# First batch's query work of a two-stage attention kernel moved into the context stage, its products from fp32 to fp32r

## The chip, the cores and the metric

The kernel is one program on one core of a Trainium2 chip. Its engines run side by side: TensorE (PE, with its weight loads as PEld), VectorE (DVE), ScalarE (ACT), GpSimd (POOL) and the sync engine (SP), which issues nearly all DMAs. The metric is the device time of one execution in microseconds; lower is better. Three executions of the kernel before took 1945.25, 1947.76 and 1950.10 us, median 1947.76 us.

## The reference

Two layers over latents `x` (4 batches x 256 rows x 512) with a context of 1601 rows of 512 per batch. The change touches the first layer's attention alone:

```
C_q  = layernorm(x) @ Wq_d                  # 512 -> 64
C_kv = ctx @ Wkv_d                          # 512 -> 32
q    = (C_q @ W_qk)  as 16 heads of 32
attn = softmax(q . C_kv / sqrt(32)) over the 1601 context rows
x    = x + attn @ (C_kv @ Wv_u as 16 heads of 32)
```

Then follow a layer norm and a product with int4 weights, a grouped attention (16 heads, 4 groups, head size 96) over context and latents, and a mixture layer. The softmax subtracts a maximum for each row of scores, so the kernel computes scores twice: once as maxima, once as exponents.

## The kernel before

There are three functions, each a block that ends when all engines have reached its end, DMAs landed.

**First stage, `context_products`.** The context is cut in 16 pieces (4 per batch, 384 rows, the last of each batch 449). For each piece PE turns it (`turn`), ACT and DVE split it into a high and a low fp32r part, and PE makes three key groups (`keys_of`, 12 products each) and three or four value groups (`values_of`, 12 products each). Weights are turned between the value groups of pieces 1 to 12 (`("w", w)`). Groups take one of four PSUM banks in turn, and before PE opens a bank it waits until the group four places back has been read (`open_bank`). ACT reads a group first and DVE after it. `turn_c` turns 32 compressed columns, which are stored in `cst_scr` as the first layer's keys. The list `groups(n)` is the order of work for all engines. In its last pieces stand the turning of the first batch's normalised rows (`("x", 0)`, `("x", 1)`, in piece 13) and `C_q` (`("cq",)`, in piece 14). SP walks its own fixed order: at the head of iteration n the load of context piece n + 2 and `load_small(n)`, then the key stores of piece n, the compressed rows of n - 1, the weight loads for n + 1, the stores of turned output weights (`wo_out`, two buffers), the value store.

**Second stage, `latent_attention_and_ffn`.** Sixteen courses s = 0 to 15, four for each batch, each for one group of four heads. `before()` stands ahead of them: eight query products of batch 0 (`("a", 0, hp)`, two heads each, fp32, stationary `wqk` of 64 partitions), 32 maxima of course 0 (`("max", 0, i)`, one product of 400 columns and one DVE reduction each), the row of the maxima (`row`), and the first six maxima of course 1. A course interleaves 13 pairs of score products with 26 other items: the maxima of the course after it, and in some courses query products (`a`), `C_q` (`cq`), normalisation, products for the third stage. `course(s)` shares these out between the scores by a fixed count. These items use a ring of four banks as well. The score products use three banks that ACT empties by exponents; `values` follow two score pairs later. The stage starts with DMAs of batch 0's keys (`cst`, 600 KB) and values (`cv`).

**Third stage, `grouped_attention`**, uses `home[0]` and two more buffers for keys. The change only renames one of them.

"Piece" and "iteration" are counted from 0. A "v tile" is a value group; "read" means that ACT and DVE have both taken what they need.

Of the kernel before, what the change touches and what calls it, by code (L numbers as in the profile page):

```python
# [8 lines left out]
ALU = mybir.AluOpType  # L9
# [119 lines left out]
def build(nc, A, out):  # L129
# [10 lines left out]
    with ExitStack() as ctx:  # L140
# [9 lines left out]
        home = [sb(f"home{i}", [P, n], F32R) for i, n in enumerate((NK + 1, 2 * GC, NK + 1))]  # L150
        with ExitStack() as early:
            def weight(name, cols, dt=F32R):
# [6 lines left out]
                     (("bias0", [P, D]), ("wqd", [P, DC, LQ]), ("wqk", [LQ, H0, 3 * HD0]), ("wvu", [P, NG * 2, 2, HD0 + 1]),  # L159
                      ("cq", [LQ, T]))}  # L160
            context_products(nc, A, ident, negid, ps, ln, home, wkvh, wkvl, wqh, wql, w0T, w1T, *small.values(),
                             k_scr, v_scr, cst_scr, cv_scr, wo_scr)
            latent_attention_and_ffn(nc, A, ident, negid, ps, ln, home, wkvh, wkvl, wqh, wql, w0T, *small.values(),
                                     cst_scr, cv_scr, q_scr, k_scr, v_scr, x_scr)
        grouped_attention(nc, A, ident, negid, ps, ln, home, q_scr, k_scr, v_scr, x_scr, wo_scr, sum_scr, o_scr, w1T, out)

def context_products(nc, A, ident, negid, ps, ln, home, wkvh, wkvl, wqh, wql, w0T, w1T, bias0, wqd, wqk, wvu, cq,
# [15 lines left out]
    C0 = 3 * HD0  # L184

    with ExitStack() as ctx:  # L186
# [6 lines left out]
        cnat = sb("cnat", [P, 3, 3, D])  # L193
        ctail = sb("ctail", [P, D])
        xa = sb("xa", [P, TT, D])
# [7 lines left out]
        wd = sb("wd", [P, DC, HD0])  # L203
        w0i = sb("w0i", [P, DC, D], I32)
        w0s = sb("w0s", [P, DC, D // P])
        w0z = sb("w0z", [P, DC, D // P])
        w0n = w0i[:, :, :].bitcast(F32)
        xaT = w0n[:, 0:2, :].rearrange("p a (c m) -> p (a c) m", c=2)
        wo_out = sb("wo_out", [HD1, 2, 2, D], F32R)

        const = sem("const0")
        ctx_in = [sem(f"ctx_in{i}") for i in range(3)]
# [4 lines left out]
        w_small, xa_in, xa_done, step_a = sem("w_small_loaded"), sem("xa0_in"), sem("xa0_ready"), sem("dve_step0")  # L217
        done = {"act": sem("group_read_by_act"), "dve": sem("group_read_by_dve")}
# [16 lines left out]
        def groups(n):  # L235
# [16 lines left out]
        def last_reader(g):  # L252
            kind = g[0]
            if kind in ("x", "cq") or kind == "w" and F_0 <= g[1] < F_1:
                return "act"
# [40 lines left out]
        def _(sp):  # L296
# [18 lines left out]
            def load(n):  # L315
                b, p = divmod(n, NP)
                if n >= 3:
# [1581 lines left out]
```

## Time and profile before

| | us |
|---|---|
| median of three executions | 1947.76 |
| profiled execution, its own time | 1948.22 |
| its span, first to last instruction | 1946.4 |
| PE busy in the span | 1872.9 |
| DVE / ACT / POOL busy | 1019.9 / 904.3 / 655.7 |
| mean granted TensorE clock, share of full speed | 0.967 |

PE is busy 96% of the span, no other engine over 52%. A busy PE is not yet a PE at its peak: the second part of the page shows the granted clock in 40 slices, and two of them (the seventh and the eighth, 292 to 389 us) are at 0.6 and 0.8. In the timeline, each row has the start, the busy time, the engine and line, and in brackets how long the engine had been idle and what released it.

### The profile page before, as it was taken

Reading aid. Unit: us, or ns where it says so; the run is one execution under the profiler, and the core shown is the slowest. Engines: PE = TensorE matmul, PEld = TensorE weight load, DVE = VectorE, ACT = ScalarE, POOL = GpSimd, SP = SyncE. Lnnn points to the kernel's source line nnn. Section 1 sums busy time; section 2 is a strip of 40 time slices with the busy share of each in tenths; the row PEclk is TensorE's granted clock in tenths of the full one; section 3 lists DMA queues with packets and bytes.
Section 4 is the critical chain, followed back from the end, with each engine's and each line's share of the span. In section 5 each row is a group of like instructions: output and inputs, shape, how many; then the busy total and the mean of one; then the engine's idle time right before and its main releaser. Section 6 shows DMA issues by size and latency. Waiting matters only on the chain. (4 is left out here: it accounts for less than half of the span.)

```text
span 1946.4 us, 23155 instructions
## 1 busy us (share of the span) xinstructions
PE 1872.9 (96%) x8570; PEld 1337.1 (69%) x8570; DVE 1019.9 (52%) x1852; ACT 904.3 (46%) x1726; POOL 655.7 (34%) x630
## 2 busy tenths in 40 slices
PE   7999997999999999999979999999999999999998
PEld 6999894444465555555577777767777677777764
DVE  3464434667655565665635555554444645554415
ACT  2333331445334344444326666645666456655660
POOL 0000000000000000000017777755777577766770
PEclk9999996899999999999989999999999999999998
DMA  5978863000010111021058444544444355443201
GB/s 182 286 243 268 280 209 113 1 1 18 29 59 27 34 66 33 33 67 44 22 177 197 111 108 118 133 124 116 126 113 112 81 132 135 124 124 98 69 25 44
DMA packets 192950, 208.42 MB, mean 107 GB/s; under 512 B 87425, under 2 KB 157569, under 8 KB 192838
## 3 DMA queue, kind: packets, MB, share of 16 engines
q1 hardware_dynamic: 177124, 188.92, 34.1%
q10 hardware_dynamic: 15714, 18.03, 3.1%
q8 instruction: 68, 1.11, 0.2%
q14 instruction: 44, 0.36, 0.1%
HBM read 128.90 MB, written 77.94 MB: 106 GB/s over the span
## 5 line engine op out<-in xcount | busy, mean ns | idle before, releaser
L1475 POOL TENSOR_TENSOR pl<-pf,ph 128x512 fp32r<-128x512 f32 (+1 forms) x480 | 623.4, 1320 | 258.6 <-ACT pf L1669 258.6
L1666 ACT ACTIVATE ph<-ps 128x512 fp32r<-128x512 f32 (+1 forms) x480 | 288.4, 601 | 361.9 <-PE ps L1562 361.9
L1749 DVE TENSOR_REDUCE pm<-ps 128x1 f32<-128x464 f32 x480 | 307.7, 642 | 249.5 <-PE ps L1493 245.9
L1187 DVE TENSOR_REDUCE pm<-ps 128x1 f32<-128x400 f32 (+3 forms) x544 | 283.1, 572 | 96.9 <-PE ps L1020 84.0
L1080 ACT ACTIVATE pr<-ps 128x512 f32<-128x512 f32 (+1 forms) x416 | 219.1, 601 | 193.9 <-PE ps L952 192.9
L1669 ACT ACTIVATE pf<-ps 128x512 f32<-128x512 f32 (+1 forms) x480 | 289.7, 603 | 0.7 <-POOL pl L1475 0.7
L965 PE MATMUL ps<-pr,cv 128*64 128x512 f32 (+1 forms) x832 | 209.0, 618 | 0.0
L1580 PE MATMUL ps<-ph,vh 128*97 128x512 f32 (+1 forms) x480 | 193.0, 402 | 0.0
L1583 PE MATMUL ps<-pl,vh 128*97 128x512 f32 (+1 forms) x480 | 190.1, 396 | 0.8 <-POOL pl L1475 0.7
L1581 PE MATMUL ps<-ph,vl 128*97 128x512 f32 (+1 forms) x480 | 189.9, 396 | 0.0
L89 POOL TENSOR_SCALAR ln_v<-ln_mv 128x2 f32<-128x2 f32 x9 | 1.9, 214 | 507.1 <-DVE ln_mv L70 507.1
L1493 PE MATMUL ps<-kh,qh 96*128 96x464 f32 x320 | 121.3, 379 | 5.6 <-DVE pm L1749 5.6
L1560 PE MATMUL ps<-qh,kh 104*128 104x512 f32 x300 | 121.7, 406 | 0.0
L965 PEld LDWEIGHTS ps<-pr,cv 128*64 128x64 f32 (+1 forms) x832 | 51.9, 139 | 88.1 <-issue 59.9
L1583 PEld LDWEIGHTS ps<-pl,vh 128*97 128x97 f32 (+1 forms) x480 | 78.3, 163 | 36.0 <-POOL pl L1475 2.8
L930 POOL MEMSET home<- 96x1 f32 x1 | 0.1, 95 | 305.1 <-POOLq L186 305.1
L1581 PEld LDWEIGHTS ps<-ph,vl 128*97 128x97 f32 (+1 forms) x480 | 79.3, 165 | 27.1 <-issue 0.5
L1020 PE MATMUL ps<-home,ast 96*128 96x400 f32 (+1 forms) x256 | 91.1, 419 | 6.4 <-DVE pm L1187 3.2
L1580 PEld LDWEIGHTS ps<-ph,vh 128*97 128x97 f32 (+1 forms) x480 | 78.9, 164 | 25.1 <-issue 0.7
L1020 PEld LDWEIGHTS ps<-home,ast 96*128 96x128 f32 x256 | 50.3, 210 | 56.0 <-DVE pm L1187 25.8
L1020 PE MATMUL ps<-cst,ast 96*128 96x400 f32 (+1 forms) x256 | 83.1, 384 | 4.9 <-DVE pm L1187 3.5
L1020 PEld LDWEIGHTS ps<-cst,ast 96*128 96x128 f32 x256 | 46.0, 192 | 50.2 <-DVE pm L1187 28.2
(273 smaller groups left out, 3098.2 us busy)
## 6 DMA issues: line engine op xcount, KB each, us to landing
woT<-wo_turned SPq DMA_DIRECT2D x30, 768.0 KB, 6.1
v_scr<-vst SPq DMA_DIRECT2D x16, 1152.0 KB
cnat<-in_ctx_dram SPq DMA_DIRECT2D x16, 768.0 KB
q_scr<-qst SPq DMA_DIRECT2D x48, 256.0 KB, 2.5
vh<-v_scr SPq DMA_DIRECT2D x15, 672.0 KB
vl<-v_scr SPq DMA_DIRECT2D x15, 672.0 KB
home<-k_scr SPq DMA_DIRECT2D x14, 696.4 KB, 8.9
k_scr<-home SPq DMA_DIRECT2D x24, 384.0 KB, 7.8
```

The source lines that it names most:

```text
L965: mm = pe.matmul(bank(OB)[64 * half:64 * half + 64, :], cv[0:keys[kt], b % 2, kt, :], pr[0:keys[kt], n % NPR, half * BANK:(half + 1) * BAN ...
L1020: mm = pe.matmul(out[:, 0:k], queries, keys_t, start=True, stop=True)
L1080: act.activation(pr[0:keys[kt], n % NPR, half * BANK:(half + 1) * BANK], bank((2 * n + half) % SB)[0:keys[kt], :], ACT.Exp, scale=S0).then ...
L1187: dve.reduce_max(pm[:, j, ch:ch + 1], src[:, 0:(cuts if s < S else next_cuts)[ch][1]], AX)\
L1475: pool.tensor_tensor(pl[0:m, n % 2, cols], pf[0:m, half, :], ph[0:m, n % 2, cols].bitcast(F32), ALU.subtract).then_inc(plo, 1)
L1560: pe.matmul(out, kh[s % 3][:, k0:k0 + m], qh[s % 3][:, cols], start=True, stop=False)
L1580: pe.matmul(out, vh[0:m, s % 2, kt, :], ph[0:m, n % 2, cols], start=(kt == 0), stop=False)
L1581: pe.matmul(out, vl[0:m, s % 2, kt, :], ph[0:m, n % 2, cols], start=False, stop=False)
L1583: mm = pe.matmul(out, vh[0:m, s % 2, kt, :], pl[0:m, n % 2, cols], start=False, stop=(kt == KT - 1))
L1666: act.activation(ph[0:keys[kt], n % 2, cols], src, ACT.Exp, scale=S1).then_inc(phi, 1)
L1669: act.activation(pf[0:keys[kt], half, :], src, ACT.Exp, scale=S1).then_inc(exp_done, 1)
L1749: ins = dve.reduce_max(pm[:, j, ch:ch + 1], at[:, 0:cuts[ch][1]], AX)
```

## The change

- The first batch's first four query products (heads of groups 0 and 1), all 32 maxima of course 0 and their row go into the first stage: `a` into piece 13, maxima 8 to piece 13, 12 to piece 14, 12 to piece 15, the row after the last turning. `before()` is gone. The other four query products of batch 0 and the first maxima of course 1 are now items of course 0.
- The keys of batch 0 are loaded from `cst_scr` into a buffer of their own (`key0`) at iteration 6; queries have two tensors of two groups each (`ast0`, which also holds the turned output weights, and `ast1`).
- Query products are fp32r: `wqk` has 128 partitions, its upper half high parts and its lower half the low parts of the same weights, `cq` is written twice (partitions 0 to 63 and 64 to 127) and `cql` holds its low part. So each pair of fp32 products becomes four fp32r products, and `C_q` is computed twice, once for each half of the partitions.
- `wqk` is loaded at iteration 7 (six DMAs, where three stood at iteration 3), split by ACT and DVE after key group 2 of piece 8; the batch's rows are loaded at iteration 9 (was 2), turned in piece 11 (was 13), `C_q` comes in piece 12 (was 14). The context has two buffers of its own instead of three.

```diff
@@ context_products: groups(n)
             if n == N:
-                return [("c", N - 1)]
+                return [("c", N - 1), ("row",)]
             ws = list(weights_of(n))
-            order = [("k", n, 0), ("c", n - 1), ("k", n, 1), ("k", n, 2)]
+            first = {N - 3: [("a", hp) for hp in range(4)]}.get(n, [])
+            order = [("k", n, 0), ("c", n - 1)] + first[:1] + [("k", n, 1)] + first[1:2] + [("k", n, 2)] + first[2:3]
+            m0, m1 = {N - 3: (0, 8), N - 2: (8, 20), N - 1: (20, 32)}.get(n, (0, 0))
             for t, g in enumerate(tiles):
-                order += [g] + [("w", w) for w in ws[t:t + 1]]
-            if n == N - 3:
+                order += [g] + [("w", w) for w in ws[t:t + 1]] + (first[3:] if t == 0 else [])
+                lo, hi = [m0 + (m1 - m0) * u // len(tiles) for u in (t, t + 1)]
+                order += [("m", i) for i in range(lo, hi)]
+            if n == N - 5:
                 order += [("x", 0), ("x", 1)]
-            if n == N - 2:
+            if n == N - 4:
                 order += [("cq",)]
@@ SP
-                if n >= 3:
-                    sp.wait_ge(tp, DC * (n - 2))
+                if n >= 2:
+                    sp.wait_ge(tp, DC * (n - 1))
...
+                elif n == 6:
+                    sp.wait_ge(cs_st, 16 * NP)
+                    sp.dma_start(key0[0:HD1, 0:NC].bitcast(F32), cst_scr[0]).then_inc(key_in, 16)
+                elif n == 9:
+                    sp.wait_ge(wqk_lo, 1)
                     sp.dma_start(xa[:, :, :], A["x"][0].rearrange("(t p) d -> p t d", p=P)).then_inc(xa_in, 16)
...
-                elif n == 3:
-                    for r in range(3):
-                        sp.dma_start(wqk[:, :, r * HD0:(r + 1) * HD0],
-                                     A["L0_xattn_W_qk"].rearrange("l (h e) -> l h e", e=HD0)).then_inc(w_small, 16)
+                    sp.wait_ge(*turned(("w", F_1 - 1)))
+                    for half in range(2):
+                        for r in range(3):
+                            sp.dma_start(wqk_in[half * LQ:(half + 1) * LQ, :, r * HD0:(r + 1) * HD0],
+                                         A["L0_xattn_W_qk"].rearrange("l (h e) -> l h e", e=HD0)).then_inc(w_qk, 16)
@@ PE, first stage
+            def latent_keys(hp):
+                out = open_bank(("a", hp))
+                if hp == 0:
+                    pe.wait_ge(*read(("cq",)))
+                for j in range(2):
+                    pe.matmul(out[0:HD1, j * T:(j + 1) * T], wqk[:, 2 * hp + j, :], cq[:, :], start=True, stop=False)
+                    mm = pe.matmul(out[0:HD1, j * T:(j + 1) * T], wqk[0:LQ, 2 * hp + j, :], cql[:, :], start=False, stop=True)
+                mm.then_inc(product, 1)
+
+            def first_max(i):
+                out = open_bank(("m", i))
...
+                pe.matmul(out[:, 0:k], ast0[0:HD1, j * P:(j + 1) * P], key0[0:HD1, k0:k0 + k], start=True, stop=True)\
+                    .then_inc(product, 1)
@@ ACT, first stage
+                    elif g[0] == "a":
+                        act.wait_ge(*turned(g))
+                        if g[1] == 0:
+                            for i in range(2):
+                                act.wait_ge(o_st[i], 32 * (F_END - F_O) // 2)
+                        act.copy(ast0[0:HD1, g[1] * BANK:(g[1] + 1) * BANK], bank_of(g)[0:HD1, :]).then_inc(a_hi, 1)
...
+                    if g == ("k", 8, 2):
+                        act.wait_ge(w_qk, 16 * 6)
+                        act.copy(wqk[:, :, :], wqk_in).then_inc(wqk_hi, 1)
@@ second stage
-            extra, tail = {LEAD + 2: [("raise", s - 1)]} if s else {}, []
+            extra, tail = {LEAD + 2: [("raise", s - 1)]} if s else {5 * i + 4: [("a", 0, 4 + i)] for i in range(4)}, []
...
-            for i in range(LEAD, NI):
+            for i in range(LEAD if s else 0, NI):
                 main += extra.get(i, []) + maxima(s + 1, i, i + 1)
...
-        def before():
-            out = [("a", 0, 0), ("a", 0, 1)] + maxima(0, 0, 2)
-            for hp in range(2, 8):
-                out += [("a", 0, hp)] + maxima(0, 5 * hp - 8, 5 * hp - 3)
-            return out + [("row", 0)] + maxima(1, 0, LEAD)
...
                     for c in range(DC):
-                        mm = pe.matmul(out[0:LQ, 0:T], wqd[:, c, :], xaT[:, c, :], start=(c == 0), stop=(c == DC - 1))
+                        for half in range(2):
+                            mm = pe.matmul(out[half * LQ:(half + 1) * LQ, 0:T], wqd[:, c, :], xaT[:, c, :],
+                                           start=(c == 0), stop=(c == DC - 1))
                 elif g[0] == "a":
                     if g[1] and g[2] == 0:
                         pe.wait_ge(*read(("cq", g[1])))
                     for j in range(2):
-                        mm = pe.matmul(out[0:HD1, j * T:(j + 1) * T], wqk[:, 2 * g[2] + j, :], cq[:, :],
-                                       start=True, stop=True)
+                        pe.matmul(out[0:HD1, j * T:(j + 1) * T], wqk[:, 2 * g[2] + j, :], cq[:, :], start=True, stop=False)
+                        mm = pe.matmul(out[0:HD1, j * T:(j + 1) * T], wqk[0:LQ, 2 * g[2] + j, :], cql[:, :],
+                                       start=False, stop=True)
```

How the order moves on PE, at the border of the first two stages. Before: L490 is the last turning of the compressed rows (`turn_c`), the branches are the border, L1043 the query products, L1020 the maxima.

```order
L479 MATMUL ps<-wkvh,xl 65x416 x4
L490 MATMUL ps<-ident,cn 96x128 x3
L490 MATMUL ps<-ident,cn 96x65
L186 UNCONDITIONAL_BRANCH
L941 UNCONDITIONAL_BRANCH
L1043 MATMUL ps<-cq,wqk 96x256 x4
L1020 MATMUL ps<-home,ast 128x400 x2
L1043 MATMUL ps<-cq,wqk 96x256 x2
L1020 MATMUL ps<-home,ast 128x400
L1020 MATMUL ps<-home,ast 128x402
L1020 MATMUL ps<-home,ast 128x400 x3
```

After: L551 is a maximum of course 0 in the first stage, L557 the row, L1030 the first scores, L1099 the maxima of course 1, L1124 and L1125 the two parts of a query product.

```order
L502 MATMUL ps<-wkvh,xl 65x416 x4
L551 MATMUL ps<-key,ast 128x400 x2
L551 MATMUL ps<-key,ast 128x402
L513 MATMUL ps<-ident,cn 96x128 x3
L513 MATMUL ps<-ident,cn 96x65
L557 MATMUL ps<-ident,mx 8x128
L190 UNCONDITIONAL_BRANCH
L1019 UNCONDITIONAL_BRANCH
L1030 MATMUL ps<-ast,key 128x512 x2
L1099 MATMUL ps<-key,ast 128x400
L1030 MATMUL ps<-ast,key 128x512 x2
L1099 MATMUL ps<-key,ast 128x400 x2
```

The query products and the maxima between the border and the first scores are gone, and three of the maxima stand behind the last v tile.

On PE in piece 14 after the change: L502 are the 12 products of a v tile, L551 the four maxima that follow each tile.

```order
L502 MATMUL ps<-wkvh,home 128x416 x4
L551 MATMUL ps<-key,ast 128x400 x3
L551 MATMUL ps<-key,ast 128x402
L502 MATMUL ps<-wkvh,home 128x416 x4
L502 MATMUL ps<-wkvl,home 128x416 x4
```

Before, v tiles stood there without anything between them.

On SP, at the head of iteration 7, first before the change, then after it: L320 and L332 are the load of context piece 9, L374 and L394 the key stores of piece 7.

```order
L391 DMA v_scr<-vst 128x2x1152
L320 DMA cnat<-in_ctx_dram 128x3x512
L374 DMA k_scr<-home 128x2x449 x2
L374 DMA k_scr<-kst 128x2x449
L331 DMA cst_scr<-cs 96x384
```

```order
L411 DMA v_scr<-vst 128x2x1152
L332 DMA cnat<-in_ctx_dram 128x3x512
L367 DMA bias<-in_L_ffn_bias_dram 128x512
L372 DMA w0i<-in_L_xattn_W_qk_dram 64x16x32 x6
L394 DMA k_scr<-home 128x2x449 x2
L394 DMA k_scr<-kst 128x2x449
```

Seven DMAs have come between the load of the context and the key stores.

## Rows read from the trace of the kernel before

**Rows 1.** The page: busy time of PE, and the granted clock in 40 slices.

```profile
PE 1872.9 (96%) x8570; PEld 1337.1 (69%) x8570; DVE 1019.9 (52%) x1852; ACT 904.3 (46%) x1726; POOL 655.7 (34%) x630
...
PEclk9999996899999999999989999999999999999998
```

**Rows 2.** Timeline, border of the stages: start, busy us, engine, line, idle before.

```profile
298.94 0.91 PE L479 MATMUL ps<-wkvh,xl 128*65 128x416 f32 x4
...
308.40 3.70 PE L1043 MATMUL ps<-cq,wqk 64*96 64x256 f32 x8 [6.57 <-PEq L186]
...
312.00 0.80 POOL L934 MEMSET cv<- 128x832 f32 x1
...
346.89 0.67 PEld L952 LDWEIGHTS ps<-ast,home 104*128 104x128 f32 x2
```

**Rows 3.** Timeline, one turn of `before()`: query product, five maxima, the next.

```profile
319.10 2.02 PE L1043 MATMUL ps<-cq,wqk 64*96 64x256 f32 x4
...
322.49 2.50 DVE L1187 TENSOR_REDUCE pm<-ps 128x1 f32<-128x401 f32 x5
...
323.75 2.02 PE L1043 MATMUL ps<-cq,wqk 64*96 64x256 f32 x4
```

**Rows 4.** Windows: length, busy of PE, PEld, DVE, ACT, POOL, PEclk, DMA share, GB/s.

```profile
18.00:20.00 2.00, 0.64 (x6) 0.40 (x5) 0.56 (x1) 0.48 (x1) 0.00 (x0) 1.00 0.99 323
...
22.00:24.00 2.00, 0.09 (x1) 0.12 (x1) 1.76 (x3) 0.50 (x2) 0.00 (x0) 0.97 0.90 334
...
352.00:353.00 1.00, 1.00 (x7) 0.35 (x8) 1.00 (x2) 0.54 (x2) 0.00 (x0) 1.00 0.00 0
...
314.00:342.00 28.00, 27.43 (x56) 14.14 (x54) 18.60 (x35) 3.49 (x6) 0.00 (x0) 0.50 0.24 71
```

**Rows 5.** Timeline, piece 13: end of one v tile, its reads, end of the next.

```profile
259.50 0.91 PE L479 MATMUL ps<-wkvh,xl 128*128 128x416 f32 x4
...
260.45 0.48 ACT L570 CAST vst<-ps 128x384 fp32r<-128x384 f32 x1 [1.80 <-PE ps L479]
...
261.43 0.25 DVE L650 COPY cn<-ps 128x96 f32<-128x96 f32 x1
...
261.78 0.91 PE L479 MATMUL ps<-wkvh,xl 128*128 128x416 f32 x4
```

**Rows 6.** Timeline of PE in courses 0 and 2: `values` (L965), a query product, a maximum.

```profile
360.08 1.94 PE L965 MATMUL ps<-pr,cv 128*64 128x512 f32 x8
...
364.17 1.94 PE L965 MATMUL ps<-pr,cv 128*64 128x512 f32 x8
...
449.43 1.94 PE L965 MATMUL ps<-pr,cv 128*64 128x512 f32 x8
...
452.33 1.10 PE L1043 MATMUL ps<-cq,wqk 64*96 64x256 f32 x4
453.36 0.45 PE L1020 MATMUL ps<-cst,ast 96*128 96x400 f32 x1
...
454.39 1.94 PE L965 MATMUL ps<-pr,cv 128*64 128x512 f32 x8
```

**Rows 7.** Timeline of PE: fp32r products of 256 columns, for the third stage.

```profile
543.71 0.63 PE L974 MATMUL ps<-xth,wqh 128*128 128x256 f32 x4
544.18 0.63 PE L974 MATMUL ps<-xth,wql 128*128 128x256 f32 x4
```

**Rows 8.** Timeline of SP's queue: loads of `wqk`, and output weights in iteration 8.

```profile
72.25 7.75 SPq L352 DMA_DIRECT2D wqk<-in_L_xattn_W_qk_dram  x3
...
171.94 6.32 SPq L387 DMA_DIRECT2D wo_turned<-wo_out  x6
```

**Rows 9.** Waits of ACT, 0 to 310 us: us in total, times, longest us.

```profile
ACT wo_out L557 <- DMA wo_turned<-wo_out: 16.7, 4, 6.5
```

**Rows 10.** Windows, iteration 7: columns as in rows 4.

```profile
140.00:158.00 18.00, 18.00 (x105) 16.56 (x105) 8.21 (x15) 5.46 (x10) 0.00 (x0) 1.00 0.72 230
```

**Rows 11.** Timeline of PE: `C_q` of batch 0, fp32.

```profile
280.87 1.94 PE L507 MATMUL ps<-w0i,wqd 128*64 128x256 f32 x8
```

More of the change, by code:

```diff
@@ L253, in last_reader @@
             kind = g[0]
-            if kind in ("x", "cq") or kind == "w" and F_0 <= g[1] < F_1:
+            if kind == "x" or kind == "w" and F_0 <= g[1] < F_1:
                 return "act"
@@ L526, in _ @@
                         latent_queries()
+                    elif g[0] == "a":
+                        latent_keys(g[1])
+                    elif g[0] == "m":
+                        first_max(g[1])
+                    elif g[0] == "row":
+                        first_row()
                     else:
@@ L675, in group @@
                     c_lo(g[1])
+                elif g[0] == "cq":
+                    dve.wait_ge(cq_hi, 1)
+                    dve.tensor_tensor(cql[:, :], bank_of(g)[0:LQ, 0:T], cq[0:LQ, :], ALU.subtract).then_inc(done["dve"], 1)
+                elif g[0] == "a":
+                    lo = ast0[2 * HD0:3 * HD0, g[1] * BANK:(g[1] + 1) * BANK]
+                    dve.wait_ge(a_hi, g[1] + 1)
+                    dve.tensor_tensor(lo, bank_of(g)[2 * HD0:3 * HD0, :], lo, ALU.subtract).then_inc(done["dve"], 1)
+                elif g[0] == "m":
+                    i = g[1]
+                    dve.wait_ge(*turned(g))
+                    dve.reduce_max(pm[:, i // KC, i % KC:i % KC + 1], bank_of(g)[:, 0:cuts[i % KC][1]], AX)\
+                        .then_inc(done["dve"], 1)
+                    if i == QT * KC - 1:
+                        dve.wait_ge(*read(g))
+                        dve.reduce_max(mx[:, :], pm[:, :, :], AX).then_inc(mx_done, 1)
+                elif g[0] == "row":
+                    dve.wait_ge(*turned(g))
+                    shift_rows(dve, ast0[HD1:HD1 + QT, 0:GC], bank_of(g)[0:QT, 0:P], negid).then_inc(done["dve"], 1)
+                if g == ("k", 8, 2):
+                    dve.wait_ge(wqk_hi, 1)
+                    dve.tensor_tensor(wqk[LQ:2 * LQ, :, :], wqk_in[LQ:2 * LQ, :, :], wqk[LQ:2 * LQ, :, :], ALU.subtract)\
+                        .then_inc(wqk_lo, 1)
             line = iter([(n, g) for n in range(N + 1) for g in groups(n)])
@@ L827, in items @@
         def items():
-            yield from before()
             for s in range(S):
@@ L1037, in ring_item @@
                     for c in range(DC):
-                        mm = pe.matmul(out[0:LQ, 0:T], wqd[:, c, :], xaT[:, c, :], start=(c == 0), stop=(c == DC - 1))
+                        for half in range(2):
+                            mm = pe.matmul(out[half * LQ:(half + 1) * LQ, 0:T], wqd[:, c, :], xaT[:, c, :],
+                                           start=(c == 0), stop=(c == DC - 1))
                 elif g[0] == "a":
@@ L1057, in ring_item @@
                 mm.then_inc(product, 1)
-            for g in before():
-                ring_item(g)
             for s in range(S):
@@ L1107, in ring_item @@
                     act.copy(qst[:, u % 2, 0, 0:width(u)].bitcast(F32R), src[:, 0:width(u)]).then_inc(qhi, 1)
-            for g in before():
-                ring_item(g)
             for s in range(S):
```

140 lines of the change are left out of this document (83 added, 57 removed).

## The prediction

> **What bounds the kernel now.** I read the page first: PE is busy 96% of the span, and the granted clock has two low slices [rows 1]. Then the windows around those slices, the timeline of the border between the first two stages, and the timelines of the places that the change touches. From 308.40 us, where the second stage begins, to 346.89, where the weights of the first score are loaded, lies `before()`: 38.5 us without one score [rows 2]. It runs in turns of 4.65 us (319.10 to 323.75), a query product and five maxima, and the clock is at 0.50, the 1.2 GHz level, although PE shows 27.4 us busy of 28 [rows 3, 4]. In each turn PE has 3.4 us of columns (4 instructions of 512 column passes, 5 of 400, at 1.2 GHz); the rest is the ring, where DVE's 2.50 us for five maxima and the ACT and DVE reads of the product follow each other. At 352 us, in the first scores, the clock is back at 2.4 GHz. So the same work costs twice there what it would cost elsewhere, and this is what the change aims at. In the first stage PE is the bound: 18.0 of 18 us in iteration 7, DVE 8.2 [rows 10]. The v tiles of piece 13 follow each other without a gap [rows 5].
>
> **The change part by part.**
>
> *The stretch that goes.* After the border the first score waits only for POOL, whose memset of `cv` takes 0.80 us [rows 2]; in the new order it comes first on POOL, then a small one. I put the first score 1.1 us behind the border: 38.5 - 1.1 = 37.4 us gone. The keys are there already; `cv` is needed four score pairs later, some 5 us, for 192 KB issued first.
>
> *What comes into pieces 13 to 15.* A v tile takes 2.28 us (259.50 to 261.78); its products end at 260.41, its reads at 261.68, so 1.27 us later [rows 5]. Behind the tile PE now opens banks for maxima, and the bank four places back decides. With three items between two tiles, the next tile waits until this one is read: 1.3 us, of which the maxima use about 0.6. With four items (piece 14), it waits for the first maximum too, one DVE reduction of 0.50 us (2.50 for five [rows 3]): 1.27 + 0.5 + 0.1 = 1.87. Piece 13: three query products between key groups, about 0.5 each, and three tiles at 1.3: 5.4. Piece 14: 3 x 1.87 = 5.6. Piece 15: three tiles at 1.3; behind the last tile only its turning and the store count, delayed by DVE's three reductions, 0.6: 4.5. Sum 15.5 us. The cheapest it can be is the columns alone, 32 x 400 and 16 x 256 at 2.4 GHz, 7 us; the dearest is that nothing overlaps, 32 reductions of 0.5 and 4 products read in turn, 22. The row (one DVE operation) lies beside the stores and the border and costs nothing; without that cover it would cost its PE, DVE and waiting time, 1.5. ACT's copy of the first query product must wait until the last turned weights are stored; I count nothing, since PE can go on for three groups, and 3 us if it can't.
>
> *Query products in fp32r.* One in fp32 takes PE 1.03 us (452.33 to 453.36) and is not hidden: two score pairs with `values` take 4.96 us with it (449.43 to 454.39) and 4.09 with maxima alone (360.08 to 364.17) [rows 6]. Four fp32r products of 256 columns take 0.47 (543.71 to 544.18) [rows 7], so each of the 24 of batches 1 to 3 gives 0.56; I take 13 us in all. Least: a unit cannot go under 4.09, and if the other stationary shape or the switch costs 0.2 more, 24 x 0.3 = 7. Most: 0.7 each with the neighbours' transitions, 17.
>
> *`C_q` twice.* Eight fp32 instructions take 1.87 us of 1.94 [rows 11], sixteen would take 3.74. But the two halves use different 64-column halves of the array, as the halves of `values` do: those are eight instructions of 512 columns in 1.94 us [rows 6], while a single one of 256 takes 0.23, so they run in pairs. Between 0 and 1.9 for each of four; I take 0.3 each, near the row of `values`, 1.3 us in all.
> The Trainium skill (TensorE: Matmul & The Clock Gate, section Part 3: Packing small matmuls) says the same of small stationary operands, that matmuls on different column groups run concurrently, with 2.38 times for three groups; by its factor the two halves would cost 0.6 more each time, 2 us in all instead of 1.3. No row here shows the case with 256 columns.
>
> *Course 0.* It gets 36 items where it had 26: six more maxima and four query products at 0.5. A unit of 4.09 us has slack, since one with four maxima and one with five take the same, so half of the maxima are free: 4 x 0.5 + 3 x 0.25 = 2.8 us. From 1 to 5. It starts at 1.2 GHz as before; before, `before()` had run ahead of it, and the clock rose 5 us into the course. From a standing start I add 0.5 us, up to 2.
>
> *DMAs.* Six loads of `wqk` come into iteration 7, ahead of the key stores. Three took SP 7.75 us [rows 8], so six about 15.5. Iteration 7 has slack: the DMA share is 0.72 of 18 us [rows 10], 5 us of transfer. Six loads need some 8 us of transfer, the bias and the rows 2.5. From iteration 8 on there is hardly any: six stores of turned weights hold SP 6.3 us [rows 8], and ACT waits 16.7 us for them in four waits, the longest 6.5 [rows 9]. What iteration 7 does not absorb arrives there, about 5 us, part of it under work in ACT's wait. I take 3 us; from 0 to 12. The split of `wqk` (1536 columns, three times the 0.5 us that ACT takes for 384 to 512, as an estimate 1.5 to 2 us on ACT and DVE each) lies under the v tiles of piece 8. Two context buffers cost nothing: SP reaches iteration n after the tiles of n - 1, when piece n has long been turned.
 The trace agrees as far as it goes, 7.75 us of issue for 384 KB.
>
> *Sum*, against the profiled execution of 1948.2 us: -37.4 - 13 + 15.5 + 2.8 + 0.5 + 1.3 + 3 = -27.3, so 1920.9. The median of the runs is 0.5 below the profiled one: 1920.5 us. Own range of this case, 1911 to 1929.
>
> **The rivals.**
>
> *The DMA queue becomes the bound of pieces 8 to 12.* The third of the `wqk` loads, not the first, sets the pace: with nearly 5 us each SP would lose 29 us, not 15.5, and the key and value stores of piece 7 would come 13 us late. PE can run about 8 us ahead on its four banks. For it: the waits of rows 9, which already reach 6.5 us, and each PE gap there also sends the clock down. Against it: the share of 0.72. It costs 10 us more and 2 for the clock: 1932.
>
> *The fp32r products give nothing in place.* If a unit is held by the exponents and not by PE, the 13 us go to 3: 1930. Against it: 4.96 against 4.09 us.
>
> *The ring overlaps better.* If DVE reads maxima ahead of the tile and the tiles wait less, pieces 13 to 15 cost 9 and not 15.5: 1914. Against it: DVE keeps the order of the list.
>
> *Slower: the clock falls in pieces 13 to 15.* PE's load there drops to about 70% of its columns, which is what `before()` had, and that stayed at 0.50 for all of its length [rows 4]. If the waits behind each v tile let it fall and it doesn't rise, ten tiles and nine key groups, 43 us of work, take twice that, less 8 us that the waits absorb: 35 us more, 1956. It decides as soon as a wait of 1.3 to 1.9 us is enough for a fall. Against it: at 18 to 20 us PE is busy 0.64 us of 2 and the clock stays at 1.00; only in 22 to 24, with 0.09 us busy of 2, does it begin to fall, to 0.97 [rows 4]. And key groups follow without gaps.
> [...]
>
> **How the numbers follow.** The forecast 0.66; the DMA queue 0.17; fp32r without effect 0.05; better overlap 0.06; slower 0.06, with the clock and mishaps of its kind. The predicted time is the forecast's, 1920.5. For the range I take the better overlap and its own uncertainty at the low end, 1909, and the DMA rival with most of its spread at the high one, 1935; outside remain the clock's case and the ends of the others. A measurement of this kernel can tell about 0.3%, 6 us, from no change: faster than that in all cases but the last and the worst end of the DMA case, 0.91; within it 0.03; slower 0.06.
>
> **What would show it.** Right: the first scores about 1 us after the border; the border 18 to 20 us later than at 308.4; v tiles in piece 14 at intervals of 4.1 to 4.2 us, in piece 15 at 3.6; query products at half a microsecond or less in courses 2 to 11; a clock at 1.00 in pieces 13 to 15. Wrong: ACT's wait on the turned weights well over 20 us, or a new ACT wait on key or value stores in piece 8 (DMA rival); units with a query product still at 4.9 us; PEclk at 0.5 ahead of the border; a border later than 335 us.

## The result and the profile after

Four executions of the changed kernel took 1929.73 to 1935.98 us, median 1931.70; four of the kernel before, in the same session, had a median of 1946.62. The ratio is 0.9923, with an interval of 0.9908 to 0.9937: 15 us faster, where 27 were forecast (1920.5), and inside the range of 1909 to 1935. In a later session six more executions of the same changed kernel had a median of 1938.61 (1928.18 to 1944.83), ratio 0.9952 [0.9931, 0.9972]; the experiment with the fp32 products looks at the difference. Over the ten runs the median is 1936.8, so that the second session and the whole lie just outside the range.

The page of the changed kernel, its span 1931.3 us, its own time 1933.15, mean granted clock 0.981:

```profile
PE 1851.9 (96%) x8602; PEld 1328.5 (69%) x8602; DVE 1021.2 (53%) x1857; ACT 905.1 (47%) x1727; POOL 656.0 (34%) x630
...
PEclk9999998999999999999989999999999999999999
```

The slices at 0.6 and 0.8 of [rows 1] are one at 0.8: the long slow stretch is gone. The timeline of PE at the border (L551 maxima, L513 the turning of the compressed rows, L557 the row, L1030 the first score), which answers to [rows 2], and of POOL, whose start marks the border:

```profile
321.33 0.72 PE L551 MATMUL ps<-key,ast 96*128 96x400 f32 x3
322.90 0.56 PE L513 MATMUL ps<-ident,cn 128*96 128x128 f32 x4 [0.85 <-DVE cn L715]
324.56 0.37 PE L557 MATMUL ps<-ident,mx 128*8 128x128 f32 x1 [1.10 <-DVE mx L755]
330.96 1.22 PE L1030 MATMUL ps<-ast,key 104*128 104x512 f32 x2 [6.03 <-POOL cv L1011]
```
```profile
329.91 0.80 POOL L1010 MEMSET cv<- 128x832 f32 x1 [324.69 <-POOLq L190]
```

The first score comes 1.05 us behind the border, and the border has gone from 308.40 to 329.91: 21.5 us, where the prediction had 18 to 20. A v tile of piece 14 with its maxima, then the next tile (L502), to be read against [rows 5]:

```profile
286.71 0.92 PE L502 MATMUL ps<-wkvh,home 128*128 128x416 f32 x4
...
288.97 0.71 PE L551 MATMUL ps<-key,ast 96*128 96x400 f32 x3
290.46 0.45 PE L551 MATMUL ps<-key,ast 96*128 96x402 f32 x1 [0.78 <-DVE cn L715]
290.94 1.03 PE L502 MATMUL ps<-wkvh,home 128*128 128x416 f32 x4
```

The fourth maximum waits until DVE has taken the tile's compressed columns (L715); from tile to tile it is 4.23 us (4.35 for the next two), where 2.28 stood. In piece 15, with three maxima, it is 3.78 to 3.87. A query product is now four fp32r instructions, two with 128 rows of weights and two with 64. In piece 13 the four of these products take 1.15, 1.14, 1.06 and 1.06 us each, and not 0.47. In the courses it is 1.07 (L1124 with 128 rows of weights, L1125 with 64), and this is a whole unit, from one `values` (L1043) to the next, to be read against [rows 6]:

```profile
437.91 1.94 PE L1043 MATMUL ps<-pr,cv 128*64 128x512 f32 x8
...
440.72 0.28 PE L1124 MATMUL ps<-cq,wqk 128*96 128x256 f32 x1
440.93 0.35 PE L1125 MATMUL ps<-cql,wqk 64*96 64x256 f32 x1
441.22 0.36 PE L1124 MATMUL ps<-cq,wqk 128*96 128x256 f32 x1
441.50 0.35 PE L1125 MATMUL ps<-cql,wqk 64*96 64x256 f32 x1
441.79 0.45 PE L1099 MATMUL ps<-home,ast 96*128 96x400 f32 x1
...
442.82 1.94 PE L1043 MATMUL ps<-pr,cv 128*64 128x512 f32 x8
```

The unit is 4.91 us where [rows 6] have 4.96. These units are unlike (4.2 to 5.9 us), so each has to be compared with its own counterpart: batches 1 to 3 have 18 of them with query products and no other item but maxima. With one product (15 units) a unit is 0.04 to 0.07 us shorter after the change, with two (3 units) 0.04 to 0.07 longer, together 0.7 us less for 21 products; the median is 4.96 before and 4.90 after. Units with maxima alone are at 4.09 in both.

Windows of the changed kernel in pieces 13, 14 and 15, then shortly after the first score (length, busy time of PE, PEld, DVE, ACT, POOL, the granted clock, DMA share, GB/s):

```profile
255.00:278.00 23.00, 21.76 (x115) 18.24 (x111) 11.63 (x21) 7.46 (x14) 0.00 (x0) 1.00 0.54 169
278.00:300.00 22.00, 19.28 (x105) 17.31 (x106) 12.93 (x28) 4.97 (x9) 0.00 (x0) 1.00 0.32 117
300.00:322.00 22.00, 19.66 (x99) 17.02 (x97) 9.96 (x22) 3.89 (x8) 0.00 (x0) 1.00 0.34 125
334.00:335.00 1.00, 1.00 (x5) 0.70 (x3) 0.80 (x2) 0.56 (x3) 0.00 (x0) 0.62 1.05 393
335.00:336.00 1.00, 1.00 (x6) 0.49 (x4) 0.58 (x1) 0.59 (x2) 0.00 (x0) 1.00 1.03 387
```

The clock stays at full speed through the waits behind the tiles, and is back 4 to 5 us after the first score. `C_q`, twice as many instructions as in [rows 11], and ACT's wait on turned weights, which answers to [rows 9]:

```profile
253.35 1.95 PE L531 MATMUL ps<-w0i,wqd 128*64 128x256 f32 x16
```
```profile
ACT ast L612 <- DMA wo_turned<-ast: 18.8, 4, 5.9
```

### The profile page after: what moved, and what is told of

It is laid out like the page before. It is cut to its first block and busy times, and to the rows that moved or that the text cites. A ratio compares the mean times of both kernels' runs of the same rounds, so it can differ in the third digit from the quotient of the medians.

```text
span 1931.3 us, 23231 instructions
## 1 busy us (share of the span) xinstructions
PE 1851.9 (96%) x8602; PEld 1328.5 (69%) x8602; DVE 1021.2 (53%) x1857; ACT 905.1 (47%) x1727; POOL 656.0 (34%) x630
## 5 line engine op out<-in xcount | busy, mean ns | idle before, releaser
L1265 DVE TENSOR_REDUCE pm<-ps 128x1 f32<-128x400 f32 (+3 forms) x512 | 267.0, 572 | 92.3 <-PE ps L1099 79.4
L1043 PE MATMUL ps<-pr,cv 128*64 128x512 f32 (+1 forms) x832 | 208.3, 619 | 0.0
L1043 PEld LDWEIGHTS ps<-pr,cv 128*64 128x64 f32 (+1 forms) x832 | 51.0, 139 | 87.1 <-issue 59.5
L1099 PE MATMUL ps<-home,ast 96*128 96x400 f32 (+1 forms) x256 | 83.1, 383 | 7.0 <-DVE pm L1265 4.9
L1030 PE MATMUL ps<-ast,key 104*128 104x512 f32 (+1 forms) x208 | 76.8, 432 | 7.8 <-POOL cv L1011 6.0
L1099 PEld LDWEIGHTS ps<-home,ast 96*128 96x128 f32 x256 | 45.8, 191 | 52.1 <-DVE pm L1265 27.9
L1641 PE MATMUL ps<-home,key 104*128 104x512 f32 x180 | 73.9, 411 | 5.0 <-PEq L799 4.9
L1030 PE MATMUL ps<-ast,home 104*128 104x512 f32 (+1 forms) x208 | 75.1, 423 | 1.7
L1099 PE MATMUL ps<-key,ast 96*128 96x400 f32 x224 | 71.5, 379 | 3.5 <-DVE pm L1265 2.5
```

The source lines that it names most:

```text
L1043: mm = pe.matmul(bank(OB)[64 * half:64 * half + 64, :], cv[0:keys[kt], b % 2, kt, :], pr[0:keys[kt], n % NPR, half * BANK:(half + 1) * BAN ...
L1099: mm = pe.matmul(out[:, 0:k], queries, keys_t, start=True, stop=True)
L1265: dve.reduce_max(pm[:, j, ch:ch + 1], src[:, 0:(cuts if s < S else next_cuts)[ch][1]], AX)\
L1641: pe.matmul(out, kh[s % 3][:, k0:k0 + m], qh[s % 3][:, cols], start=True, stop=False)
```

## The experiments

The forecast failed in the price of the query products, so the first experiments ask what makes four fp32r instructions of 256 columns take up to 0.29 us each where [rows 7] have 0.12.

**Both fp32r products on 128 rows.** Low part of `C_q` on all 128 partitions, so that no weight load has 64 rows. It adds one term (low part times low part) to the sum.

```diff
-                      (... ("cq", [2 * LQ, T]), ("cql", [LQ, T]), ...)}
+                      (... ("cq", [2 * LQ, T]), ("cql", [2 * LQ, T]), ...)}
-                    mm = pe.matmul(out[...], wqk[0:LQ, 2 * hp + j, :], cql[:, :], start=False, stop=True)
+                    mm = pe.matmul(out[...], wqk[:, 2 * hp + j, :], cql[:, :], start=False, stop=True)
-                    dve.tensor_tensor(cql[:, :], bank_of(g)[0:LQ, 0:T], cq[0:LQ, :], ALU.subtract)
+                    dve.tensor_tensor(cql[:, :], bank_of(g)[:, 0:T], cq[:, :], ALU.subtract)
```

> The changed kernel, with the low part of C_q kept on all 128 partitions, so that both fp32r products of a query product have a stationary of 128 rows (it adds the product of the two low parts, which is tiny). In the changed kernel a query product takes 1.15 us, 0.29 for each instruction, where I had forecast 0.47. Theory A, the alternation of 128 and 64 rows costs about 0.17 us at each switch: a query product takes 0.5 to 0.6 us, the 28 of courses 0 to 15 give 14 to 18 us, with the four of the first stage 2 more, some of it taken by the exponents' pace: median near 1916, 1912 to 1920. Theory B, the stationary of 96 columns or the moving of cq is slow by itself: 0.29 stays and the time stays at 1930 to 1933. Theory C, the query products are hidden behind the exponents: they become shorter, the time does not change.

Measured: 1917.97 us (1913.39 to 1918.76), ratio to the kernel before 0.9851 [0.983, 0.9871]. Timeline of PE in this kernel:

```profile
432.83 0.28 PE L1124 MATMUL ps<-cq,wqk 128*96 128x256 f32 x1
432.95 0.28 PE L1125 MATMUL ps<-cql,wqk 128*96 128x256 f32 x1
433.06 0.28 PE L1124 MATMUL ps<-cq,wqk 128*96 128x256 f32 x1
433.18 0.28 PE L1125 MATMUL ps<-cql,wqk 128*96 128x256 f32 x1
433.31 0.35 PE L1099 MATMUL ps<-home,ast 96*128 96x400 f32 x1
```

The same four instructions now take 0.48 us, the 0.47 of [rows 7], and a unit with them 4.28 us (median of the same 18); over the 21 products the units lose 13.5 us against the changed kernel. The columns and the order are the same; what has changed is the height of two of the four weight loads, and of `cql` with it. Theory B falls (0.12 apart, not 0.29), and so does Theory C (the units became shorter too). The weight loads (PEld) show where the time goes. First the load for a 64-row product and the product itself in the changed kernel, then the same for its 128-row counterpart here:

```profile
440.93 0.16 PEld L1125 LDWEIGHTS ps<-cql,wqk 64*96 64x96 f32 x1 [0.28 <-issue]
440.93 0.35 PE L1125 MATMUL ps<-cql,wqk 64*96 64x256 f32 x1
```
```profile
432.83 0.16 PEld L1125 LDWEIGHTS ps<-cql,wqk 128*96 128x96 f32 x1
432.95 0.28 PE L1125 MATMUL ps<-cql,wqk 128*96 128x256 f32 x1
```

With all heights at 128 the load starts with the product before, 0.12 us ahead of its own. At a change to or from 64 rows it isn't ahead (440.93 for both, and within 0.01 us the same at 441.21, 441.50 and 441.79), so the load is no longer hidden. Why it isn't made ahead there, no run shows. Theory A, the change of height, is what fits.

**Two changes of height instead of four.** The order is high, low, low, high.

```diff
-                for j in range(2):
-                    pe.matmul(out[...], wqk[:, 2 * hp + j, :], cq[:, :], start=True, stop=False)
-                    mm = pe.matmul(out[...], wqk[0:LQ, 2 * hp + j, :], cql[:, :], start=False, stop=True)
+                for j, low in ((0, 0), (0, 1), (1, 1), (1, 0)):
+                    w, q = (wqk[0:LQ, 2 * hp + j, :], cql[:, :]) if low else (wqk[:, 2 * hp + j, :], cq[:, :])
+                    mm = pe.matmul(out[...], w, q, start=(low == j), stop=(low != j))
```

> The changed kernel with the four products of a query product in the order high, low, low, high: two switches between 128 and 64 rows inside instead of three. Theory A (a switch costs 0.17 us): 0.98 instead of 1.15 us, the neighbouring low products 0.12 apart; 28 times 0.17 is up to 5 us: 1927 to 1931. Theory B2 (any stationary of 64 rows costs 0.29, switch or not): no change in pace or time.

Measured: 1927.68 us (1925.32 to 1928.66), ratio 0.9904 [0.9885, 0.9922]. Timeline of PE:

```profile
435.63 0.28 PE L1125 MATMUL ps<-cq,wqk 128*96 128x256 f32 x1
435.84 0.47 PE L1125 MATMUL ps<-cql,wqk 64*96 64x256 f32 x2
436.24 0.36 PE L1125 MATMUL ps<-cq,wqk 128*96 128x256 f32 x1
436.43 0.34 PE L1099 MATMUL ps<-home,ast 96*128 96x400 f32 x1
```

0.80 us, and the unit 4.53 (median of the 18). With no change to or from 64 rows the product takes 0.47, with two 0.80, with four 1.07: 0.17 us for each of the first two and 0.14 for each of the others. It fell by more than was expected. One expectation failed: the two low products are 0.20 us apart (435.84 and 436.03) and not 0.12, though the weights of the second were loaded ahead (435.92). So the price of a change is spread over the next two products. Theory B2, that 64 rows cost 0.29 with or without a change, falls all the same.

**The query products in fp32, all else moved.** This tells what the move alone is worth.

```diff
-                    pe.matmul(out[...], wqk[:, 2 * hp + j, :], cq[:, :], start=True, stop=False)
-                    mm = pe.matmul(out[...], wqk[0:LQ, 2 * hp + j, :], cql[:, :], start=False, stop=True)
+                    mm = pe.matmul(out[...], wqk[0:LQ, 2 * hp + j, :], cq[0:LQ, :], start=True, stop=True)
```

> The changed kernel with its query products in fp32 again (one product of 64 rows where two of fp32r were), all that was moved stays moved. If the fp32r form gives nothing, as 1.15 us against 1.03 says, the time stays within 3 us of the changed kernel's 1932 and the whole gain belongs to the move. The courses with four query products are 1.7 us shorter after the change, which speaks for 5 us: then 1935 to 1938. My forecast of 13 us for this part would give 1945.

Measured: 1941.07 us (1932.18 to 1942.92, ten runs), ratio 0.9966 [0.9951, 0.998]. The product is `435.75 1.10 PE L1124 ... x4`, ended by the next maximum at 436.78: 1.03 us, as before; the unit 4.95 (median of the 18), and each unit is within 0.01 us of the same unit of the kernel before. By the medians fp32r would be worth 9 us, by the paired units 0.7 for 21 products, 0.8 for 24. (The 2 us in the next expectation come from medians over unlike units.) The two kernels were run again, in one session:

> The changed kernel once more, unaltered, on one chip with the fp32 version below, to settle how much the fp32r products as the change has them are worth. In the traces a unit of a course with a query product takes 4.87 us in this kernel and 4.95 in the fp32 version; over 24 products that is 2 us in place, and four products in the first stage are 0.1 us dearer each. Theory F (only that is real, the 9 us between the two medians were chance between runs): this kernel 2 to 4 us below the fp32 version, both with the same mean clock. Theory G (the fp32 version also has the clock fall more often: 0.977 mean against 0.981 in the runs so far, and 0.004 of 1934 us is 7.5 us): 7 to 10 us below it, again with 0.003 to 0.004 more clock. I expect G, 1932 us here.

> The changed kernel with its query products in fp32, as in the experiment with the fp32 products before, once more beside the unaltered changed kernel. Theory F: 2 to 4 us above it at the same clock, about 1935. Theory G: 7 to 10 us above it at a mean clock lower by 0.003 to 0.004, about 1941.

Measured: the unaltered changed kernel 1938.61 us (1928.18 to 1944.83), ratio 0.9952 [0.9931, 0.9972]; the fp32 version 1936.46 (1931.04 to 1941.76), ratio 0.9951 [0.9934, 0.9968]. No difference can be seen, so Theory G falls; 1 or 2 us, as by Theory F, are below what was resolved. Over both sessions the medians are 1936.8 (10 runs) and 1940.3 (16 runs), with mean clocks of 0.9785 and 0.9778. The fp32r products, as the change has them, are worth about 1 us by the units, and the medians can't say more.

The repeat also shows what differs from execution to execution. These are windows of the changed kernel in its first profiled execution (span 1931.3), then in the second (span 1943.0):

```profile
324.00:335.00 11.00, 4.41 (x12) 3.38 (x12) 3.85 (x7) 2.70 (x7) 2.46 (x4) 0.53 0.68 207
...
503.00:504.00 1.00, 0.36 (x1) 0.10 (x1) 0.96 (x3) 0.66 (x2) 0.00 (x0) 1.00 0.03 8
505.00:509.00 4.00, 4.00 (x14) 2.29 (x14) 1.50 (x4) 2.17 (x4) 2.73 (x14) 0.57 0.00 0
```
```profile
199.00:207.00 8.00, 6.81 (x22) 6.71 (x23) 7.10 (x16) 3.65 (x7) 0.00 (x0) 0.57 0.75 224
...
329.00:347.00 18.00, 12.36 (x31) 7.07 (x32) 5.46 (x9) 4.92 (x10) 2.47 (x4) 0.53 0.71 199
...
512.00:513.00 1.00, 0.24 (x3) 0.20 (x2) 0.97 (x3) 0.34 (x1) 0.00 (x0) 1.00 0.03 8
513.00:521.00 8.00, 8.00 (x26) 4.27 (x26) 5.31 (x16) 2.17 (x4) 2.74 (x14) 0.57 0.00 0
```

Adding up (1 - granted clock) over all windows of 1 us in which it was under 0.97 gives 36.9 us in the first execution and 52.5 in the second, as the mean clocks of 0.981 and 0.973 also say. The difference is 15.6, that of the spans 11.7. The same kernel has more or fewer such stretches, and they are longer or shorter. They are large enough for the scatter; that they are all of it is not shown, since part of each stretch is time in which PE waits anyway.

**The maxima two by two.** In pieces 14 and 15 maxima also stand behind the key groups, and never more than two between tiles.

```diff
-            m0, m1 = {N - 3: (0, 8), N - 2: (8, 20), N - 1: (20, 32)}.get(n, (0, 0))
+            ms = iter([("m", i) for i in {N - 3: range(0, 6), N - 2: range(6, 18), N - 1: range(18, 32)}.get(n, ())])
...
+            order = [("k", n, 0), ("c", n - 1)] + first[:1] + ahead() + [("k", n, 1)] + first[1:2] + ahead() \
+                + [("k", n, 2)] + first[2:3] + ahead()
             for t, g in enumerate(tiles):
-                lo, hi = [m0 + (m1 - m0) * u // len(tiles) for u in (t, t + 1)]
-                order += [("m", i) for i in range(lo, hi)]
+                order += two()
```

> The changed kernel with the 32 maxima of the first stage spread two to each value and key group of pieces 13 to 15 (6, 12, 14) instead of three or four behind value groups alone. Same work. If the waits for the ring of four banks make these pieces long, as ten waits of about 0.77 us in the trace say, they go: 8 us less, in pieces 14 and 15 2 to 2.5 us between the end of one tile's products and the next tile's start become 0.5; median near 1924. If the maxima cost PE time itself (three in 0.71 us), the time stays within 2 us.

Measured: 1927.68 us (1924.66 to 1928.90), ratio 0.9903 [0.9884, 0.9922]. Timeline of PE in piece 14 and at the border (L509 v tiles, L558 maxima, L1037 the first score):

```profile
289.93 0.91 PE L509 MATMUL ps<-wkvh,home 128*128 128x416 f32 x4
...
292.19 0.53 PE L558 MATMUL ps<-key,ast 96*128 96x400 f32 x2
292.56 0.92 PE L509 MATMUL ps<-wkvh,home 128*128 128x416 f32 x4
...
324.82 1.22 PE L1037 MATMUL ps<-ast,key 104*128 104x512 f32 x2 [6.67 <-POOL cv L1018]
```

From tile to tile it is 2.63 us instead of 4.23, with no wait: two maxima cost their 0.37. The first score comes at 324.82 where it was at 330.96, 6.1 us earlier. From `C_q` to the first score it is 71.0 us instead of 77.6, so 6.6 us of what pieces 13 to 15 cost were waits on the ring and not work. The larger part was work: 32 maxima of 0.185 us (5.9) and the four query products (4.4).

**The weights in two loads of whole rows.** Pieces of 2 KB instead of six loads in pieces of 128 bytes; ACT's copy repeats each head three times.

```diff
-                        for r in range(3):
-                            sp.dma_start(wqk_in[half * LQ:(half + 1) * LQ, :, r * HD0:(r + 1) * HD0], ...)
+                        sp.dma_start(w0n[half * LQ:(half + 1) * LQ, 0, :], A["L0_xattn_W_qk"])
```

> The changed kernel with W_qk loaded in two DMAs of whole 2 KB rows instead of six with pieces of 128 bytes; ACT and DVE make the three copies when they split it. DMA theory: the 2.4 us by which piece 13 starts later than before, beyond the moved turning and C_q, come from these loads; ACT's waits on the turned weights and value stores (29.7 us in the changed kernel, 23.8 before) fall back and 2 to 3 us are gone: 1929. Rival: the lag comes from the clock or from the moved rows load; no change within 1 us.

Measured: 1934.80 us (1932.47 to 1936.16), ratio 0.9926 [0.9912, 0.9941]. `C_q` comes at 251.43 where it was at 253.35, and the first score at 329.01 where it was at 330.96. That looks like 1.9 us for the loads, but SP's queue shows otherwise, first in the changed kernel, then in this one (L332 is the load of a context piece, at iteration 3; L372 and L371 are the loads of `wqk`, at iteration 7):

```profile
71.98 0.47 SPq L332 DMA_DIRECT2D cnat<-in_ctx_dram  x1
...
141.79 9.20 SPq L372 DMA_DIRECT2D w0i<-in_L_xattn_W_qk_dram  x6
```
```profile
70.08 0.47 SPq L332 DMA_DIRECT2D cnat<-in_ctx_dram  x1
...
139.88 2.04 SPq L371 DMA_DIRECT2D w0i<-in_L_xattn_W_qk_dram  x2
```

This execution was 1.9 us ahead at 70 us, 70 us before the edit does anything, and was 1.9 us ahead at `C_q` still. In the nine profiles of kernels with six loads `C_q` starts at 252.3 to 257.1, so 1.9 us is within what one execution differs from the next; PE's waits between 130 and 250 us add up to 6.9 us with six loads and 6.8 with two. ACT's wait on turned weights is listed as 16.4 us and not 18.8, but a fourth wait at the same line, of 2.4 us, is only put down to another releaser. So the DMA theory falls: the six loads hold SP for 9.2 us instead of 2.0, and cost nothing that can be seen. The rival in the expectation, no change, holds; whether the moved load of the rows or something else makes the lag was not separated.

**The wait on POOL moved to the first values.** The scores of course 0 don't need the memset of `cv`.

```diff
@@ scores
-                if kt == 0 and s == 0:
-                    pe.wait_ge(const, 2)
@@ values
+                if kt == 0 and s == 0:
+                    pe.wait_ge(const, 2)
```

> The changed kernel with PE's wait for POOL's memsets of cv moved from the first scores to the first values. The first scores start 1.0 us earlier after the border and the stage ends 1 us earlier: 1931. If what comes after (values waiting for cv, exponents) is late anyway, nothing.

Measured: 1932.22 us (1928.42 to 1938.04), ratio 0.9919 [0.9893, 0.9944]. From the row to the first score it is 5.36 us (323.50 to 328.86) instead of 6.40, so the first score comes 1.0 us earlier, as expected; the time shows nothing.

**All four together.** Its edit is those of the tall products, the spread maxima, the two loads and the late wait.

> The changed kernel with four edits together: both fp32r products with 128 rows, the maxima spread two to a group, W_qk loaded in whole rows, and the wait for POOL at the first values. If they add up (15, 8, 2, 1 us): 1906, 1901 to 1911. If they cover the same waits: 1912 to 1918.

Measured: 1908.04 us (1907.46 to 1909.44), ratio 0.9791 [0.9777, 0.9806]. The first score comes at 321.95. And without the two loads and the late wait:

> Low part of C_q on all 128 partitions and the maxima of the last pieces spread two by two, without the two-DMA load of the weights and without the later wait on POOL: what the last two are worth in the combined version of 1908.0 us. Both were worth nothing alone in the medians (1934.8 and 1932.2 against 1931.7). If they are worth nothing here too: 1908 to 1910. Rival: the 1.9 us that the loads took in the first stage now show, since less hides them, and the late wait gives its 1 us: 1911 to 1913.

Measured: 1912.67 us (1904.54 to 1915.56, four runs), ratio 0.982 [0.9799, 0.984]; first score at 321.36, its profiled span 1902.7. The intervals overlap. From `C_q` to the first score it is 67.8 us with all four and 68.9 without the two loads and the late wait. The loads are long over there, so this is the late wait: its 1 us is there in the stage, and the earlier first score comes from ahead of `C_q`. In the time, what the two small edits are worth stays open. Either version beats both kernels, by more than the change itself did.

**The stretch before the scores, with its maxima doubled.** This one is an edit of the kernel before. It asks whether the clock stays low in `before()` because PE waits there. Each maximum of `before()` is multiplied twice into its bank.

```diff
+                    if s == 0 or s == 1 and i < LEAD:
+                        pe.matmul(out[:, 0:k], queries, keys_t, start=True, stop=True)
                     mm = pe.matmul(out[:, 0:k], queries, keys_t, start=True, stop=True)
```

> The kernel before the change, with each of the 38 maxima products ahead of the first course run twice into the same bank (more work for PE, same result). There PE is at 1.2 GHz for 35 us though shown busy 98%; its columns fill 73% of the time at that clock. Theory D, it is the share of columns that keeps the clock low: with 5 x 0.33 us more in each turn PE is full, the clock rises to 2.4 GHz within the stretch, and the stretch becomes shorter or stays, 30 to 38 us, although it has more work: 1940 to 1947. Theory E, the clock stays at 1.2 GHz whatever the share: each turn goes from 4.65 to about 6.2 us, the stretch from 38.5 to 50 us, time 1958.

Measured: 1952.71 us (1949.35 to 1954.98, ten runs), ratio 1.0025 [1.0014, 1.0036]. Windows of this kernel in `before()` and in course 0:

```profile
320.00:325.00 5.00, 5.00 (x14) 4.00 (x14) 2.83 (x6) 0.58 (x1) 0.00 (x0) 0.50 0.00 0
...
340.00:345.00 5.00, 5.00 (x14) 3.54 (x13) 2.80 (x7) 0.58 (x1) 0.00 (x0) 0.50 0.00 0
...
355.00:360.00 5.00, 5.00 (x21) 2.50 (x20) 2.73 (x6) 2.96 (x7) 0.00 (x0) 1.00 0.00 0
```

PE is busy 5.00 of 5 us and the clock stays at 0.50, the 1.2 GHz level, until the scores of course 0, whose first is at 353.03. A turn of `before()` took 5.59 us (319.95 to 325.54) instead of the 4.65 of [rows 3], and its columns at 1.2 GHz make 5.04 us of that (4 x 512 and 10 x 400), where they made 3.4 of 4.65. So a turn filled far better did not raise the clock, and Theory D falls as far as this edit could fill it. Theory E had the clock right and the price too high: a turn of 6.2 us and 1958 were expected.

## Why the prediction was right in its range, and wrong in one term

- **The stretch that goes: -37.4 us, right.** First score 1.05 us behind the border, forecast 1.1.
- **Query products in fp32r: -13 us, wrong by its size, and this is the step that failed.** The forecast put "four fp32r products of 256 columns take 0.47" from [rows 7] in place of 1.03, where both products of the row have weights of 128 rows. The change alternates 128 and 64 rows. It took 1.07, and the paired units give 0.7 us for 21 products, 0.8 for the 24. The least value that the prediction allowed for "the other stationary shape or the switch", 7 us, was too high also; a unit still at 4.9 us stood among the prediction's own signs of an error. The tall version shows that the idea behind the term was right: its units are 14.2 us shorter than before over 21 products, 16 us for 24, more than the 13 forecast.
- **Pieces 13 to 15: +15.5 us, measured 19.0.** From the first key product of a piece to that of the next, as in the three rows below, and 321.48 for the end of the last v tile: piece 13 is 23.1 us long (+8.2 against its old length without the turning of the rows, forecast 5.4), piece 14 21.3 (+6.1 without `C_q`, forecast 5.6), the last to its end +4.7 (4.5). The ring waits came nearly as forecast (4.23 to 4.35 us for a tile against 4.1 to 4.2, and 3.8 to 3.9 against 3.6); 2.4 of the 2.8 us missing in piece 13 are the four query products at 1.06 to 1.15 instead of 0.5.

```profile
255.23 0.97 PE L489 MATMUL ps<-xh,wkvh 128*128 128x384 f32 x4
...
278.31 0.97 PE L489 MATMUL ps<-home,wkvh 128*128 128x384 f32 x4 [0.77 <-DVE cn L715]
...
299.64 1.09 PE L489 MATMUL ps<-xh,wkvh 128*128 128x450 f32 x4
```

- **`C_q` twice: +1.3 us, measured 0.** Sixteen instructions in 1.95 us, eight in 1.94 [rows 11]. Neither the 0.3 us taken for each nor the 0.6 of the prediction's second estimate is there (which, four times, would be 2.4 and not 2).
- **DMAs: +3 us, measured 2.6, but not by the loads.** The first key product of piece 13 comes 5.3 us later; 2.7 of these are the turning of the rows and `C_q`, which now stand ahead of it. The prediction's working fails here though its number is near: six loads held SP for 9.2 us and not 15.5, and two loads in their place changed nothing in PE's waits. Those waits, from 130 to 250 us, went from 4.7 to 6.9 us for a reason that stays open. ACT's wait on the turned weights rose from 16.7 to 18.8 us in four waits, the longest of them 5.9, and a wait on the value stores of 2.4 us came in at 185 us, a piece later than the prediction's sign; the two-load version has it too. So the rival that the queue becomes the bound did not happen as it was priced. A part of it can be seen in the second execution: PE waits 2.8 us until 200.19, the clock is at 0.57 from 199 to 207 us, and `C_q` comes 3.8 us later than in the first.
- **Course 0 and the clock: +3.3 us, measured 4.6** from first score to the next course's row. The clock was back 4.5 us after the first score in this execution. In the second one it took 12 us, and the course cost 8.1.
- **Rival of a falling clock in pieces 13 to 15: did not happen**, 1.00 in all three windows, PE busy 19.3 to 21.8 of 22 to 23 us. This is against the rival's own premise, that a ring wait behind each tile is enough for a fall.
- **Sum.** -37.4 + 19.0 + 0 + 2.6 + 4.6 - 0.8 = -12.0; the profiled execution is 15.1 shorter than that of before. The 3 us left are within what the clock does from one execution to the next: behind 400 us, (1 - granted clock) adds up to 34.3 us before and 28.4 after. That scatter, 12 us between two profiles of one kernel, also means that the 15 us of the first comparison (9 in the second) fit this sum better than they could prove it: the terms are shown by the rows, not by the medians.
- **Luck.** The errors of the terms add up to 15 us, and all but 1.7 of them go the same way. That the first median still lay in the range, 3 us from its end, is owed to the session: the second median, 1938.61, does not.

The rival "fp32r without effect because the exponents pace a unit", at 1930, came close to the measured time, but by another mechanism: units did shrink, to 4.28 us, as soon as the product itself did.

## What to carry to other kernels

Before a row from another place is used as the price of a matmul, compare the height of its weights with that of its neighbours, not only its columns and type: padding or duplicating a short operand to full height can be worth more than halving the passes. Filler items between groups that share a ring of banks should be counted against the ring: two between tiles cost their columns, three or four cost a wait each time. And a difference of less than about 10 us in this kernel should be read from repeated units in the trace, each paired with its counterpart, with medians only beside them. When an instruction comes earlier after an edit, look first whether the execution was already ahead at a place that the edit does not touch.

## What was not expected of the hardware

- A change to or from weights of 64 rows costs TensorE 0.14 to 0.17 us at 2.4 GHz, because the next weights are not loaded ahead of their product; between 128 and 96 rows it does not happen (433.18 to 433.31 in the tall version). The busy time of one instruction hides it (0.28 to 0.36 us shown in all cases; the starts tell, 0.12 against 0.20 to 0.29 apart).
- In `before()` with its maxima doubled the trace shows TensorE busy without a gap for 25 us at 1.2 GHz (320 to 345), and it was not given the higher clock. What differs between that work (fp32 products of 64 rows, maxima of 96 rows) and the first scores and values, after which the clock rose, was not separated.
- The clock can stay low through full work: at 505 to 509 us and at 513 to 521 in the windows above PE was busy for the whole stretch at a mean clock of 0.57. Just ahead of both falls it had been waiting, busy 0.36 and 0.24 of 1 us (503 to 504, 512 to 513), while the waits of 0.78 us behind the v tiles brought no fall.
- `C_q` for both halves of the partitions takes the time of one half (1.95 against 1.94 us), where the forecast had allowed 0.3 for it.
